# Splitting VectorE's part of each layer norm in two, with the read of the first values' product inside the second norm

## The reference

```python
# layer 0, per graph
h = gat(x, adj, W1, a1); h = gat(h, adj, W2, a2)
h = ln(x + h) * g_ln1 + b_ln1                                       # norm 0
x = ln(h + relu(h @ w_ff1 + b_ff1) @ w_ff2 + b_ff2) * g_ln2 + b_ln2 # norm 1
# layer 1
attn = softmax(q k^T / sqrt(32))                                    # 8 heads
out = sum over r of (attn * (adj == r)) @ (x @ Wv[r] + bv[r])
y = ln(x + out @ Wo + bo) * g1 + beta1                              # norm 2
out = ln(y + gelu(y @ W1 + b1) @ W2 + b2) * g2 + beta2              # norm 3
```

## Time and profile before

| | |
|---|---|
| time, median of 3 runs | 3150.95 us (3150.66 to 3151.95) |
| profiled execution, its own time | 3147.39 us |
| its span | 3145.6 us |
| busy: PE, ACT, DVE, POOL | 3038.5, 2431.9, 2225.3, 1880.5 us |
| granted TensorE clock | 0.992 of full speed |
| memory traffic | 30 GB/s over the span |

### The profile page before, as it was taken

How to read it: one execution, slowest core, us unless ns; L and a number is a source line. 1 busy time by engine, 2 the same in 40 slices (tenths; PEclk the granted TensorE clock), 3 DMA queues, 4 the chain that set the end, 5 groups by cost and what they waited for, 6 DMA issues and landing times.

```text
span 3145.6 us, 78504 instructions
## 1 busy us (share of the span) xinstructions
PE 3038.5 (97%) x26980; PEld 2743.2 (87%) x26980; DVE 2225.3 (71%) x4975; ACT 2431.9 (77%) x6218; POOL 1880.5 (60%) x1747
## 2 busy tenths in 40 slices
PE   5799999999999999999999999999999999999997
PEld 5788888888888888889889889889889889889885
DVE  4567677777777777777777777777777777777763
ACT  3578878878878778778778787787787787787774
POOL 3365665665665665665665665666666666666664
PEclk8999999999999999999999999999999999999998
DMA  4000100100100100100100100100100100100100
GB/s 143 25 22 24 33 27 23 33 27 23 33 27 23 33 27 23 33 27 23 33 27 23 33 27 23 33 27 23 33 27 23 33 27 23 33 26 24 33 12 14
DMA packets 101943, 93.54 MB, mean 30 GB/s; under 512 B 14736, under 2 KB 101008, under 8 KB 101776
## 3 DMA queue, kind: packets, MB, share of 16 engines
q1 hardware_dynamic: 101904, 93.00, 9.8%
HBM read 76.17 MB, written 16.78 MB: 30 GB/s over the span
## 4 chain that ended last, share of the span: by engine, by line
PE 91%; DVE 7%; issue 1%; ACT 1%; POOL 0%; DVEq 0%; DMA 0%; POOLq 0%; SPq 0%; ACTq 0%
PE ps_f L288 11%; PE ps_f L289 10%; PE ps_f L290 10%; PE ps_ao L485 7%; PE ps L475 6%; PE ps L288 5%; PE ps L289 5%; PE ps L290 5%; PE ps L465 4%; PE ps_ao L288 4%; PE ps_ao L530 4%; PE ps_g L288 3%; PE ps_g L289 3%; PE ps_g L290 3%; PE ps_ao L289 3%; PE ps_ao L290 3%
## 5 line engine op out<-in xcount | busy, mean ns | idle before, releaser
L1024 POOL TENSOR_TENSOR hid_lo<-hid_full,hid_hi 128x512 fp32r<-128x512 f32 x512 | 674.0, 1317 | 406.7 <-ACT hid_hi L646 387.5
L288 PE MATMUL ps_f<-down_w_hi,hid_hi 128*128 128x256 f32 x2048 | 590.4, 288 | 1.2 <-POOL hid_lo L1024 0.9
L1001 POOL TENSOR_TENSOR rstd<-vareps,neg_half 128x2 f32<-128x2 f32 x256 | 218.1, 852 | 611.9 <-DVE vareps L819 611.9
L289 PE MATMUL ps_f<-down_w_lo,hid_hi 128*128 128x256 f32 x2048 | 572.8, 280 | 0.0
L290 PE MATMUL ps_f<-down_w_hi,hid_lo 128*128 128x256 f32 x2048 | 572.6, 280 | 0.0
L663 ACT ACTIVATE prob<-ps,s_least 128x256 f32<-128x256 f32 x1024 | 468.6, 488 | 6.1 <-DVE s_least L867 5.2
L867 DVE TENSOR_REDUCE s_least<-ps 128x4 f32<-128x1024 f32 x256 | 309.4, 1209 | 141.1 <-PE ps L465 141.1
L288 PEld LDWEIGHTS ps_f<-down_w_hi,hid_hi 128*128 128x128 f32 x2048 | 385.1, 188 | 23.2 <-issue 19.9
L289 PEld LDWEIGHTS ps_f<-down_w_lo,hid_hi 128*128 128x128 f32 x2048 | 386.0, 188 | 0.0
L290 PEld LDWEIGHTS ps_f<-down_w_hi,hid_lo 128*128 128x128 f32 x2048 | 384.7, 188 | 0.0
L646 ACT ACTIVATE hid_hi<-hid_full 128x512 fp32r<-128x512 f32 x512 | 323.4, 632 | 16.7
(11 more groups left out here) (158 smaller groups left out, 9436.3 us busy)
## 6 DMA issues: line engine op xcount, KB each, us to landing
adj_in<-adj_keys SPq DMA_DIRECT2D x128, 256.0 KB, 2.8
xT_in<-x_features SPq DMA_DIRECT2D x64, 256.0 KB, 2.8
norm<-x_nodes SPq DMA_DIRECT2D x64, 256.0 KB, 2.7
out_nodes<-norm SPq DMA_DIRECT2D x64, 256.0 KB, 2.2
row_vectors<-all_row_vectors SPq DMA_DIRECT2D x1, 1536.0 KB, 11.7
raw_up<-L_w_ff SPq DMA_DIRECT2D x1, 1024.0 KB, 8.2
raw_down<-L_w_ff SPq DMA_DIRECT2D x1, 1024.0 KB, 10.7
raw_v<-L_Wv SPq DMA_DIRECT2D x4, 256.0 KB, 10.6
```

Source lines behind the costliest of these rows:

```text
L288: nc.tensor.matmul(ps_out, left[0], right[0], start=first, stop=False)
L289: nc.tensor.matmul(ps_out, left[0], right[1], start=False, stop=False)
L1024: pool.tensor_tensor(hid[1][:, 2 * m:2 * m + 2, :], hid_full[:, 2 * m:2 * m + 2, :], value(hid[0][:, 2 * m:2 * m + 2, :]), ALU.subtract).t ...
```

## The change

`dve_norm` ends behind the two bn_stats; what followed (the wait for both, the gate, the union, the two reduces) becomes a function of its own, `dve_spread`. Behind norms 0, 2 and 3 it is called at once. For norm 1, `dve_v(b, 0)` stands between the two, and `dve_rec(b, 1, 1)` comes behind the second. No other engine's stream is changed.

```diff
--- before.py
+++ after.py
@@ -810,6 +810,9 @@
             dve.wait_ge(*ysum[n](g, 1))
             for i in range(C):
                 dve.bn_stats(stats[n][:, i, :], y[:, i, :]).then_inc(stat_set[n].sem, 1)
+
+        def dve_spread(dve, g, n):
+
             dve.wait_ge(*stat_set[n](g, 2))
             dve.sem_inc(gate_v.sem, 1)
             for i in range(C):
@@ -936,8 +939,11 @@
             if ff0:
                 dve_norm(dve, a, 1)
             if att1:
+                dve_v(dve, b, 0)
+            if ff0:
+                dve_spread(dve, a, 1)
+            if att1:
                 dve_rec(dve, b, 1, 1)
-                dve_v(dve, b, 0)
             if gat:
                 dve_gat_score(dve, c, 1)
             if att1:
@@ -959,6 +965,7 @@
                 dve_fence(dve, e)
             if gat:
                 dve_norm(dve, c, 0)
+                dve_spread(dve, c, 0)
             if nxt:
                 dve_gat_in(dve, e)
                 if isinstance(t, int) and t == -3:
@@ -980,6 +987,7 @@
                 dve_mask_more(dve, b, 1)
             if ff1:
                 dve_norm(dve, d, 3)
+                dve_spread(dve, d, 3)
             if ff0:
                 dve_adj_top(dve, a)
             if att1:
@@ -990,6 +998,7 @@
                     dve_bias_setup(dve, 0)
             if att1:
                 dve_norm(dve, b, 2)
+                dve_spread(dve, b, 2)
 
 
         def pool_gat_in(pool, g):
```

## The result

The changed kernel takes 3170.55 us, the kernel before 3151.45 beside it: a ratio of 1.0057 (95% interval 1.0046 to 1.0068), so 18 us more (14 to 21). The forecast was 3121 us, faster. What came is the first rival, rstd losing the tie for the port (what VectorE and GpSimd can't use at the same time), at nearly its price in the round.

A forecast was written before the change was run, and what follows sets the result against it. TensorE was taken to bound the kernel, through its wait for line 848's v_sb. The turn 0.47 us earlier in 63 rounds gave 29.6 us: profiled 3147.39 to 3117.8, median 3150.95 to 3121 us; range 3112 to 3149, 0.8 of the chance.

The forecast's parts named there:

- the first rival: Norm 1: rstd waits for the score's end, the turn 0.22 us later a round, 14 us, 3165; chance 0.16.
- What bounds the kernel: TensorE, busy 97% of the span; its wait for line 848's v_sb, 63 times 0.58 us, was to be won.
- The read: Line 848 on VectorE: starts at 1541.25, not 1541.96, and TensorE's second product comes 0.71 us earlier.
- The norm up to rstd's start: Norm 1 on VectorE and GpSimd: union 0.57 behind the read's start, gate taken as free, rstd at 1542.34.
- that rival: Gate before norm 1's union costs 0.15 as today: gain only 0.23, 14.5 us, 3136.5; chance 0.14 shared with port kept.
- The tie: Norm 1: score starts at 1542.33, rstd at 1542.34; rstd was taken as unhindered, 0.70 us.
- the row of lines 790 and 1024: Nearest row to a tie: line 790 started 0.01 before GpSimd's hid_lo; GpSimd took its usual 1.29, VectorE 1.57.
- The rival's price: If rstd loses the tie at norm 1: centre takes 0.36, the turn is 0.22 later, 63 x 0.22 = 14 us.
- The sum, had rstd been free: Norm 1's turn at 1544.58, not 1545.05: 0.47 us in each of 63 rounds, 29.6 us, centre taking 0.20.
- Cover: Fence's load, second v_sb and store stay hidden, 0.24 of the fence's idle time left; rival, gain eaten there: 0.06.
- The rule of the Trainium skill: VectorE with two SBUF inputs and GpSimd reading SBUF share a port pair; whichever starts first holds it, the other blocks.

The follow-up runs named there:

- one operation between: Changed kernel with one small VectorE reduce, result unused, between s_rec and the score: 1.0063 to the kernel before, 47.77 us a round.
- the score from PSUM: Changed kernel in its own order, the second attention's score reading one of its two operands from PSUM: 0.9882 to the kernel before, 3118.97 us.
- three between: Changed kernel with three small VectorE reduces, results unused, between s_rec and the score: 0.9886 to the kernel before, 3115.36 us.
- the halves: Changed kernel with the first operation of the second attention's score as two of 128x256: 0.9972 to the kernel before, 3143.33 us.

## Why the prediction was wrong, step by step

- *What bounds the kernel*, and the wait to be won: right. The wait for v_sb is gone.
- *The read*: right to 0.04. The second product is at 2.17 from the sum and not 2.84, so 0.67 earlier; 0.71 was forecast. The read started at 1.42 as forecast, but took 0.69 and not 0.66.
- *The norm up to rstd's start*: right (2.54 from the sum, 2.51 forecast). The union starts 0.61 behind the read (0.57 forecast), and the gate costs nothing, which puts that rival out.
- *The tie*: wrong, and this is the step that failed. The sum took rstd as unhindered, 0.70 with a centre of 0.20 behind it; they took 1.21 and 0.37, and the turn came at 5.38 from the sum where 4.75 was forecast. I set the score's start at 0.01 ahead of rstd's, and that came true (0.02). I then chose the outcome by the row of lines 790 and 1024 because it was the nearest in time. It is another operation of GpSimd, and the run with one operation between shows that the score wins against rstd even 0.02 behind it. Why line 1024 had the port from 0.01 behind and rstd not from 0.02 ahead, no run here shows. rstd of norm 3 beside line 832, 0.10 apart, told the truth, and the trace of before had a row nearer still, which I didn't use: rstd beside the score of line 769 itself, in the round of the start that the earlier trace rows is from.

```profile
88.27 0.68 DVE L769 SCALAR_TENSOR_TENSOR score<-score 128x512 f32<-128x512 f32 x1
88.38 1.15 POOL L1001 TENSOR_TENSOR rstd<-vareps,neg_half 128x2 f32<-128x2 f32 x1 [11.47 <-DVE vareps L819]
```

  There was also a tie with rstd itself, in every round: v_sb at 1541.96, rstd at 1541.97, and rstd took 0.70. But v_sb reads one operand from PSUM, and the score none; the run with the score from PSUM shows that this is what counts. The point from which it turns lies between 0.02 and 0.09 behind rstd's start. I had given this a chance of 0.16; with rows that pointed to opposite sides it should have been near one half, and with the row above over it.
- *The rival's price*: right. Forecast 0.22 us a round, 0.21 to 0.22 measured; rstd 1.23 forecast, 1.21 measured; centre 0.36 and 0.37; the turn in effect 5.44 from the sum, 5.38 and 0.05 of slower first transposes measured.
- *From the price to the time*: 63 x 0.21 = 13 us, and the medians lie 19 apart (18 by the ratio, 14 at its lower end). The rest fits the steps of TensorE's up products: the two first profiles lie 23.1 us apart, 13.2 of it the turn and 56 x 0.155 = 8.7 the long steps. How the steps were spread over the executions that were only timed, and how long their start took, isn't known, so the rest of the medians' difference is argued and not shown.
- *The sum, had rstd been free*: right. The runs with three between and with the score from PSUM take 46.87 and 46.85 with short steps against 47.33, 0.46 and 0.48 less than before where the sum gave 0.47, and centre falls from 0.52 to 0.20 in the gap, as it said. The forecast of 3121 us is nearly the time of the version with three small operations between, 3115.
- *Cover*: the fence, the second v_sb and the store took nothing back. With rstd free, all of it arrived in the round.
- *The rule of the Trainium skill*, page "SBUF — State Buffer", section "SBUF: two separate sides", that a VectorE operation with two SBUF inputs and a GpSimd operation that reads SBUF exclude each other: the run with one operand from PSUM agrees, 0.70 against 1.21. That whichever starts first has the port agrees with the changed kernel, where the score's record is 0.02 earlier; but with one operation between, the score's record was 0.02 later and it won, so the starts of the records can't be taken for it. That it is held for the whole instruction holds for the score (rstd 0.56 behind its end), not for rstd: with three between, the score started 0.15 into rstd's 0.70 and took its own 0.68.

## What to carry to other kernels

When an order is changed, list for each tiny GpSimd operation on a path what VectorE does at its start, and where that operation's operands lie: one with both operands in SBUF there cost 0.5 us, where the three small operations that put it off cost 0.17 (one, of 0.04, was not enough). Where two engines arrive within a tenth of a microsecond, the trace of before can't say who wins; price both sides, share the chance, and look for a row with the same two operations, in the rounds of the start and the end too, not for the smallest distance. And a gap opened on purpose can be worth more than the move itself.

## What the hardware showed that I had not expected

- Two SBUF operands are not the only thing that holds rstd up. In norm 0 of the kernel before, in nearly every round, a cast of VectorE from one SBUF tile to another starts 0.10 ahead of rstd, and rstd takes 0.87, to 0.55 behind the cast's end:

```profile
1509.85 0.42 DVE L750 CAST gT_hi<-xT_in 128x512 fp32r<-128x512 f32 x1
1509.95 0.87 POOL L1001 TENSOR_TENSOR rstd<-vareps,neg_half 128x2 f32<-128x2 f32 x1 [0.42 <-DVE vareps L819]
```

- rstd of 2 elements a partition behaves as if it needed the port only near its start: it ends 0.56 us behind the release, and an operation of VectorE that starts 0.09 behind it no longer disturbs it. With the score at 0.02 behind it was held for 1.26.
- The port is handed over between two operations of VectorE that follow each other without a gap: rstd 0.94 beside the halves, 1.21 beside the whole.
- The steps of one stretch of matmuls, 36 in a round behind the start of the loop's body, were 113 or 118 ns at the same full granted clock, with the one or the other for all but a few rounds in seven of the twelve profiles, and mixed in five (in the run with the score from PSUM they alternate from round to round, 29 and 29 of 58). This is worth up to 9 us of 3150. The up product of the GELU block stepped by 118 ns in every round of every profile. What sets the steps stays open.
